# A four-layer model with a mixture of experts on one core: the router's lists by scatters instead of one-hot sums

## The chip, the cores and the metric

The kernel runs on one core of one Trainium2 chip. The metric is device microseconds for one execution. Five engines run side by side: PE (TensorE, matrix products), DVE (VectorE), ACT (ScalarE), POOL (GpSimd) and SP (SyncE, which here only starts DMAs). Each works through its own instructions in order and waits on semaphores for the others.

## The reference, cut to what matters

Four layers follow one another on 2048 rows (4 sequences of 512) of 512 features, each with a residual and a layernorm. Layers 1 and 2 (lightning attention, gated feed-forward) are not touched.

```python
# layer 3, the gated layer: q, k, v, g are four projections of x
g = sigmoid(x @ Wg.T + bg)
y = q * cumsum(k * v, axis=1) * g
x = layernorm(x + y)
# layer 4, the experts (E = 32, K = 8 chosen, the first 4 "primary")
logits = x @ gate_weight.T
probs  = softmax(logits)
top, idx = top_k(probs, 8);  w = top / sum(top)
sim[e, e] = 1
prim, sec = idx[:, :4], idx[:, 4:]
cand = sim[sec[:, :, None], prim[:, None, :]]
best = max(cand, -1);  best_primary = prim[argmax(cand, -1)]
new_sec = where(best < 0.5, sec, best_primary)
combine = sum(one_hot([prim, new_sec]) * w)          # rows x 32 weights
for e in range(32):
    g, u = split(x @ Wgu[e].T);  y += (silu(g) * u) @ Wd[e].T * combine[:, e]
x = layernorm(x + y)
```

## The kernel before

The rows are 16 tiles of 128, and four batches (b or q, 0 to 3) of four tiles. The program has these stages: attention, feed-forward (to 666.65 us in the trace), the **gated layer**, the **router's rest**, the **experts**, the final layernorm.

**The gated layer** is a loop over 16 steps `s`, with q = s // 4 and et = s % 4 (a quarter of the features). PE computes four projections of 12 matmuls each (k, v, q, g: `gate_proj(s, 0..3)`, L745), and between them `back(s-1)` (L761), which turns the last step's product round into bank 4. ACT copies the projections out (kC, then qC, then gC by a sigmoid); DVE makes k·v and its running sum `cumC`; POOL multiplies q by g (L1772) and then by `cumC` (L1777). After four steps a batch has its residual; DVE takes its mean and variance (`norms`), POOL makes 1/std and -mean/std (`shifts`, L1761 to L1767), ACT writes the normalised tile (`high_half`, L1541), POOL its low half (`x_low`, L1686), PE turns both round (`norm_transposes`, L768, through L551).

**The router** of batch q-1 runs beside the steps of batch q. PE computes the logits from the normalised, turned tiles (`logits`, L773, 48 small matmuls). DVE finds the eight best of 32 by softmax values (`choices`); PE turns the second choices round and multiplies by a block-diagonal similarity matrix (L789, L796); DVE picks, for each of the four first choices in turn, the similarity (L1212, L1213), then the new choices and the weights (`combine`); PE ranks each row among the rows of its expert (`ranks`, L799); DVE makes places of it (`places`, L1241).

**The lists.** The experts work on blocks of 128 rows, 159 blocks in all, and a block needs the list of its rows. For each batch and each of its 32 (tile, choice) pairs, DVE writes a one-hot of the column times the row's number (`one_hots`, L1266, up to 512 wide), POOL or ACT (in turns, L1786, L1561 with L1567) a one-hot of the place, and PE adds their product into bank 7 (`slot_sums`, L815). A short tail turns bank 7 into the table of blocks (`tables_ready`), and POOL starts the first gather of rows (L1819). The lists of batches 0 and 1 are made within the loop, those of 2 and 3 behind it.

**The experts.** POOL gathers a block's rows (L1819), PE multiplies, and POOL adds the result to memory by an indirect scatter (L1826); 159 of each. The change leaves this stage alone.

The order on every engine is the order in which the code is written; there is no scheduler.

## Time and profile before

| | us |
|---|---|
| time, median of 3 runs | 1586.79 (1586.19 to 1589.04) |
| the profiled execution's own time | 1585.89 |
| its span in the trace | 1584.0 |
| busy of the span: PE | 1448.3 (91%) |
| DVE | 952.9 (60%) |
| POOL | 776.5 (49%) |
| ACT | 732.3 (46%) |
| gated layer, to the end of its last projection | 666.65 to 871.20 |
| router's rest, to the first matmul of the experts | 871.20 to 955.90 |
| experts | 955.90 to 1570 |

PE is busy in nine tenths of nearly every fortieth of the span, except where the router's rest lies. So there are two kinds of place: those in which a microsecond on PE is a microsecond of time, and the router's rest, in which PE waits for others.

### The profile page before, as it was taken

Reading aid. Unit: us, or ns where it says so; the run is one execution under the profiler, and the core shown is the slowest. Engines: PE = TensorE matmul, PEld = TensorE weight load, DVE = VectorE, ACT = ScalarE, POOL = GpSimd, SP = SyncE. Lnnn points to the kernel's source line nnn. Section 1 sums busy time; section 2 is a strip of 40 time slices with the busy share of each in tenths; the row PEclk is TensorE's granted clock in tenths of the full one; section 3 lists DMA queues with packets and bytes.
Section 4 is the critical chain, followed back from the end, with each engine's and each line's share of the span. In section 5 each row is a group of like instructions: output and inputs, shape, how many; then the busy total and the mean of one; then the engine's idle time right before and its main releaser. Section 6 shows DMA issues by size and latency. Waiting matters only on the chain.

```text
span 1584.0 us, 33491 instructions
## 1 busy us (share of the span) xinstructions
PE 1448.3 (91%) x11191; PEld 820.2 (52%) x11192; DVE 952.9 (60%) x1858; ACT 732.3 (46%) x1326; POOL 776.5 (49%) x691
## 2 busy tenths in 40 slices
PE   5999999999999999999998358999999999999990
PEld 2566666544444444445454215666666666666650
DVE  7877777776757666634988883444444444444435
ACT  6544433555464645444446442444444444444443
POOL 3565544530010202044445536777777777777655
PEclk9999999999999999999999668999999999999995
DMA  6323111269776868531101444888989898876767
GB/s 242 107 81 107 27 40 26 77 219 315 238 255 232 265 222 268 179 139 54 55 3 54 158 165 93 185 183 166 202 177 206 177 196 186 162 108 96 177 76 230
DMA packets 102991, 243.45 MB, mean 154 GB/s; under 512 B 21481, under 2 KB 23049, under 8 KB 101904
## 3 DMA queue, kind: packets, MB, share of 16 engines
q1 hardware_dynamic: 67312, 183.08, 35.0%
q0 software_dynamic: 35616, 59.58, 23.0%
q8 instruction: 34, 0.56, 0.1%
q14 instruction: 29, 0.24, 0.0%
HBM read 158.92 MB, written 101.71 MB: 165 GB/s over the span
## 4 chain that ended last, share of the span: by engine, by line
PE 68%; DVE 16%; issue 6%; POOL 4%; ACT 3%; DMA 2%; SPq 0%; DVEq 0%; POOLq 0%; ACTq 0%
PE bank L894 20%; PE bank L915 11%; PE bank L562 8%; PE bank L706 6%; PE bank L712 6%; PE bank L735 6%; PE bank L885 5%; PE bank L904 2%; ACT ARENA L1395 1%; POOL ARENA L1695 1%; DVE ARENA L1032 1%; POOL ARENA L1690 1%; DVE ARENA L1266 1%; DVE ARENA L985 1%; PE bank L551 1%
## 5 line engine op out<-in xcount | busy, mean ns | idle before, releaser
L894 PE MATMUL bank<-ARENA,XT 128*128 x1908 | 364.2, 327 | 2.2 <-issue 1.1
L1826 POOL DMA_INDIRECT accs<-X,WA x159 | 252.5, 1588 | 98.8 <-issue 34.7
L894 PEld LDWEIGHTS bank<-ARENA,XT 128*128 128x128 f16 x1908 | 180.4, 98 | 124.2 <-issue 8.2
L1356 DVE COPY XT<-bank 128x1024 f16<-128x1024 f16 x159 | 109.9, 691 | 182.3 <-PE bank L885 181.1
L1819 POOL DMA_INDIRECT XT<-x_rows,WA x159 | 166.5, 1047 | 87.0 <-issue 39.8
L1395 ACT ACTIVATE ARENA<-ARENA 128x512 f16<-128x512 f32 (+2 forms) x128 | 89.3, 709 | 245.5 <-DVE ARENA L1114 134.1
L915 PE MATMUL bank<-ARENA,XT 128*128 x795 | 197.4, 379 | 0.9 <-issue 0.9
L1649 ACT ACTIVATE XT<-bank 128x192 f32<-128x192 f32 x159 | 52.5, 330 | 287.7 <-PE bank L894 287.7
L562 PE MATMUL bank<-XT,STG 128*128 128x512 f16 x640 | 151.8, 385 | 4.6 <-DVE ARENA L1160 4.3
L1677 POOL TENSOR_TENSOR rstd<-mv,mhalf 128x1 f32<-128x1 f32 x28 | 8.7, 309 | 258.2 <-DVE mv L964 258.2
L1395 ACT ACTIVATE XT<-bank 128x384 f16<-128x384 f16 (+2 forms) x207 | 125.7, 607 | 9.5 <-PE bank L551 9.0
L562 PE MATMUL bank<-WA,XT 128*128 128x512 f16 (+1 forms) x732 | 127.1, 327 | 2.4 <-DVE ARENA L1013 1.6
L735 PE MATMUL bank<-ARENA 128*128 128x512 f16 x512 | 121.0, 379 | 3.5 <-DVE ARENA L1120 3.4
L706 PE MATMUL bank<-XT,WA 128*128 (+1 forms) x512 | 122.6, 383 | 1.0 <-issue 1.0
L1366 DVE SCALAR_TENSOR_TENSOR XT<-bank,XT 128x192 f32<-128x192 f32 x159 | 66.4, 418 | 95.0 <-ACT XT L1649 91.8
L712 PE MATMUL bank<-XT,ARENA 128*128 (+1 forms) x512 | 121.7, 381 | 0.0
L1686 POOL TENSOR_TENSOR ARENA<-X,ARENA 128x512 f16<-128x512 f32 (+1 forms) x48 | 66.6, 1401 | 88.5 <-ACT ARENA L1395 88.5
L885 PE MATMUL bank<-ident,XT 128*128 128x128 f16 x1272 | 97.8, 220 | 5.5 <-DMA XT<-x_rows,WA 5.5
L915 PEld LDWEIGHTS bank<-ARENA,XT 128*128 128x128 f16 x795 | 71.7, 98 | 57.3 <-issue 1.4
L562 PEld LDWEIGHTS bank<-XT,STG 128*128 128x128 f16 x640 | 62.1, 99 | 74.8 <-DVE ARENA L1160 5.6
L885 PEld LDWEIGHTS bank<-ident,XT 128*128 128x128 f16 x1272 | 85.0, 98 | 25.7 <-issue 6.0
L1395 ACT ACTIVATE X<-bank 128x512 f32<-128x512 f32 x159 | 93.1, 586 | 2.1 <-PE bank L915 2.1
(245 smaller groups left out, 2369.6 us busy)
## 6 DMA issues: line engine op xcount, KB each, us to landing
w_scratch<-WA SPq DMA_DIRECT2D x64, 640.0 KB, 3.9
ARENA<-w_scratch SPq DMA_DIRECT2D x64, 640.0 KB
ARENA<-w_exp SPq DMA_DIRECT2D x48, 640.0 KB, 5.2
WA<-w_exp SPq DMA_DIRECT2D x16, 640.0 KB, 5.1
ARENA<-ARENA SPq DMA_DIRECT2D x64, 128.0 KB, 2.3
accs<-ARENA SPq DMA_DIRECT2D x20, 256.0 KB, 3.1
X<-x SPq DMA_DIRECT2D x4, 1024.0 KB, 6.6
ARENA<-wc SPq DMA_DIRECT2D x8, 512.0 KB, 6.0
```

Source lines behind the costliest of these rows:

```text
L562: mm = pe.matmul(dst, wa(a, k), wb(b, k), start=n == 0, stop=n == 3 * KD - 1)
L706: mm = pe.matmul(bank[0][:, :], Wg[:, n % KD, m * P:(m + 1) * P], XT[:, n // KD, n % KD, tk], start=n == 0, stop=n == 2 * KD - 1)
L712: mm = pe.matmul(bank[1 + m % 2][:, :], Wu[:, n % KD, m * P:(m + 1) * P], XT[:, n // KD, n % KD, tk], start=n == 0, stop=n == 2 * KD - 1)
L735: mm = pe.matmul(bank[4 + tt][:, :], fB[:, m % 2, a, tt * P:(tt + 1) * P], Wd[:, m, :], start=m == 0 and a == 0, stop=m == NM - 1 and a == 1)
L885: mm = pe.transpose(d[:, c * P:(c + 1) * P], xg[k.u % NG].bitcast(F16)[:, c * P:(c + 1) * P], ident16[:, :])
L894: mm = pe.matmul(d, xTb[k.u % 2][:, a * KD + kd, :], weights(sl, b, kd * 2 * DFF, 2 * DFF), start=(a, b, kd) == (0, 0, 0), stop=(a, b, kd) ...
L915: mm = pe.matmul(d, hT[k.u % 2][:, c, :], weights(sl, j, c0, DIM), start=n == 0, stop=n == 4)
L1356: dve.tensor_copy(xTb[k.u % 2].rearrange("p c n -> p (c n)"), bank[k.u % 2][:, :].bitcast(F16)).then_inc(xt_sb, 1)
L1395: return act.activation(dst, src, ACT.Copy, scale=scale)
L1686: pool.tensor_tensor(hl[:, 1, :], tile(t), hl[:, 0, :], ALU.subtract).then_inc(x_lo, 1)
L1819: pool.indirect_dma_start(xg[i % NG], None, xrows, bass.IndirectOffsetOnAxis(blkidx[:, i:i + 1], 0), bounds_check=TOK - 1, oob_is_err=Fals ...
L1826: pool.indirect_dma_start(accs, bass.IndirectOffsetOnAxis(blkout[:, i:i + 1], 0), yD[i % 8], None, compute_op=ALU.add).then_inc(y_out[i % ...
```

## The change

The functions keep their batches; what each engine does for a batch and where it stands is written anew.

- **Logits.** The normalised tiles are no longer turned round for the router (they still are for the first of the five groups, which feeds the gated layer itself). The scores are sums over the unnormalised residual: the layer's input times the gate weights (`input_logits`, before the third projection of a batch's step et = 1) plus, step by step, the layer's product times the gate weights (`layer_logits`, 4 float32 matmuls behind each `back`), all added up in bank 3. The mean is taken off with the gate weights' column sums (`gate_sums`, `csneg`); 1/std goes into the exponent of the eight best alone (`exponents`), so that the choice itself waits for no `shifts`.
- **Second choices.** First and second choices are both turned round (8 transposes, not 4), similarities are compared among the 32 experts with a priority matrix added (12 float32 matmuls, not 4), and DVE gets the new choices in nine operations.
- **Product.** POOL multiplies q by the running sum (one operation a step, L1800 of the new numbering), DVE multiplies by g (`product`).
- **Lists.** For batches 0 to 2 POOL writes each row's number to its place in a list in memory: `dispatch`, 32 indirect scatters a batch, each of 128 single float32 numbers, 96 in all. Batch 3 keeps 32 one-hots (DVE 53, ACT 11 pairs); two indirect gathers fetch the blocks' rows of the list (`listed`), and two matmuls add them in bank 7.
- **The rest.** The last batch's weights are made on POOL behind the scatters; constants come in two DMAs, the zeros of `accs` in four wide ones; four experts' weights are loaded within the loop.

```diff
@@ DVE @@
+            def product(s):
+                dve.wait_ge(gc_sb, s + 1)
+                dve.wait_ge(a1_ready, s + 1)
+                if s >= 2:
+                    dve.wait_ge(at_ready, s)
+                dve.tensor_tensor(aC[:, s % 2, :], a1C, gC, ALU.mult).then_inc(a_ready, 1)
...
+            def exponents(b):
+                dve.wait_ge(ln_rstd, 2 * NT + (b + 1) * TB)
+                step(dve.tensor_tensor(top8[:, :, 1:TOPK], top8[:, :, 1:TOPK], top8[:, :, 0:1].to_broadcast([P, TB, TOPK - 1]), ALU.subtract))
+                step(dve.memset(top8[:, :, 0:1], 0.0))
+                dve.tensor_tensor(top8, top8, rstd[:, :, 1:2].to_broadcast([P, TB, TOPK]), ALU.mult).then_inc(exp_in, 1)
@@ POOL @@
             def product(s):
-                pool.wait_ge(gc_sb, s + 1)
                 pool.wait_ge(qc_sb, s + 1)
-                pool.tensor_tensor(a1C, qC, gC, ALU.mult).then_inc(a1_ready, 1)
-                pool.wait_ge(a1_ready, s + 1)
                 pool.wait_ge(cum_ready, s + 1)
...
-                pool.tensor_tensor(aC[:, s % 2, :], a1C, cumC, ALU.mult).then_inc(a_ready, 1)
...
+                pool.wait_ge(a_ready, s)
+                pool.tensor_tensor(a1C, qC, cumC, ALU.mult).then_inc(a1_ready, 1)
+
+            def dispatch(b, lo, hi):
+                if lo == 0:
+                    pool.wait_ge(list_ready, b + 1)
...
+                for i in range(lo, hi):
+                    t = b * TB + i // TOPK
+                    pool.indirect_dma_start(slot_list, bass.IndirectOffsetOnAxis(places_i[b][:, i:i + 1], 0), pay[:, t:t + 1], None,
+                                            bounds_check=EXPERTS * TOK - 1, oob_is_err=False).then_inc(list_out, 16)
...
             for s in range(BATCH * KD):
                 q, et = s // KD, s % KD
...
+                if et == 0 and q >= 2:
+                    dispatch(q - 2, 14, 20)
+                if et == 1 and q >= 1:
+                    norm_shifts(q)
...
+                    dispatch(q - 2, 28, 32)
+                if et == 3 and q >= 1:
+                    dispatch(q - 1, 4, 10)
                 product(s)
                 if et == 0 and q >= 2:
...
+                    dispatch(q - 2, 20, 24)
+                if et == 1:
+                    low_halves(q)
+                if et == 1 and q >= 2:
+                    dispatch(q - 2, 24, 28)
+                if et == 2 and q >= 1:
+                    dispatch(q - 1, 0, 4)
+                if et == 3 and q >= 1:
+                    dispatch(q - 1, 10, 14)
+            dispatch(2, 14, 18)
+            norm_shifts(BATCH)
+            dispatch(2, 18, 24)
+            low_halves(BATCH)
+            dispatch(2, 24, 32)
+            pool.wait_ge(wts_ready, BATCH)
...
+            for g, rows in enumerate((P, NBLK - P)):
+                pool.indirect_dma_start(listed[0:rows, g, :], None, list_rows, bass.IndirectOffsetOnAxis(listidx[0:rows, g:g + 1], 0),
+                                        bounds_check=LISTROWS - 1, oob_is_err=False).then_inc(list_in, 16)
@@ PE @@
+            def layer_logits(s):
+                for tt in range(TB):
+                    mm = pe.matmul(bank[3][:, tt * EXPERTS:(tt + 1) * EXPERTS], aC[:, s % 2, tt * P:(tt + 1) * P], gw32[:, s % KD, :],
+                                   start=False, stop=s % KD == KD - 1 and tt == TB - 1)
...
                 gate_proj(s, 0)
-                if et == 1 and q >= 2:
-                    ranks(q - 2)
-                if et == 2:
-                    norm_transposes(q, 1)
+                if s == 2:
+                    norm_transposes(1)
                 gate_proj(s, 1)
...
+                if s == 1:
+                    gate_sums()
...
+                if et == 1:
+                    if q >= 1:
+                        choice_transposes(q - 1)
+                    input_logits(q)
+                if et == 2 and q >= 1:
+                    ranks(q - 1)
                 gate_proj(s, 2)
                 if s > 0:
                     back(s - 1)
...
+                    layer_logits(s - 1)
+                if et == 1 and q >= 1:
                     similarities(q - 1)
...
                 gate_proj(s, 3)
...
-                if et == 2 and q >= 1:
-                    logits(q - 1)
-                if et == 3 and q >= 2:
-                    slot_sums(q - 2)
@@ ACT, between kC and qC @@
                 if et == 1:
-                    for tt in range(TB):
-                        high_half(q, tt)
...
+                    if q >= 1:
+                        exponentials(q - 1)
+                    high_half(q, 0)
+                    high_half(q, 1)
+                    if q >= 1:
+                        second_copy(q - 1)
+                        first_copy(q - 1)
+                    high_half(q, 2)
+                    high_half(q, 3)
```

Three places of the order follow, before and after apart. The first is POOL's, in the last quarter of the gated layer (q = 3), before: L1686 are the low halves, L1772 and L1777 the product, L1786 the one-hots of places.

```order
L1686 TENSOR_TENSOR ARENA<-X,ARENA 128x512 [waits x_hi] x4
L1772 TENSOR_TENSOR ARENA<-ARENA 128x512 [waits qc_sb,gc_sb]
L1777 TENSOR_TENSOR ARENA<-ARENA 128x512 [waits at_ready,cum_ready,a1_ready]
L1786 TENSOR_SCALAR ARENA<-WA 128x128 [waits list_ready]
L1786 TENSOR_SCALAR ARENA<-WA 128x128 x7
```

The same place after: L1800 is POOL's product, L1809 the scatters (`dispatch`), L1790 to L1794 the `shifts` of one tile (four such threes follow one another, three of them behind these rows).

```order
L1809 DMA slot_list<-WA 81920x1 [waits list_ready]
L1809 DMA slot_list<-WA 81920x1 x9
L1800 TENSOR_TENSOR ARENA<-ARENA 128x512 [waits a_ready,cum_ready,qc_sb]
L1809 DMA slot_list<-WA 81920x1 x10
L1800 TENSOR_TENSOR ARENA<-ARENA 128x512 [waits a_ready,cum_ready,qc_sb]
L1809 DMA slot_list<-WA 81920x1 x4
L1790 TENSOR_TENSOR rstd<-mv,mhalf 128x1 [waits ln_stat]
L1792 TENSOR_TENSOR rstd<-rstd,mhalf 128x1 [waits g_step]
L1794 TENSOR_SCALAR rstd<-mv,rstd 128x1 [waits g_step]
```

Of the 8 one-hots a step nothing is left, and 24 scatters stand between a batch's list and the next `shifts`; 8 more follow the low halves.

POOL again, from the last `shifts` to the first gather of the experts, after (L1714 low halves, L1862 to L1870 the last batch's weights, L1874 the gathers of `listed`):

```order
L1809 DMA slot_list<-WA 81920x1 x6
L1714 TENSOR_TENSOR ARENA<-X,ARENA 128x512 [waits x_hi] x4
L1809 DMA slot_list<-WA 81920x1 x8
L1862 TENSOR_TENSOR WA<-WA 128x1024 [waits mask_ready,wts_ready]
L1865 TENSOR_TENSOR WA<-WA 128x512 [waits g_step]
L1867 TENSOR_TENSOR WA<-WA 128x4x64 [waits g_step]
L1870 TENSOR_TENSOR WA<-WA 128x128 [waits cw_out1,g_step]
L1874 DMA WA<-slot_list,WA 128x128 [waits list_out,list_ready]
L1874 DMA WA<-slot_list,WA 31x128
```

The gathers of the list stand behind all scatters and behind the weights.

PE at a batch's router work, before (step et = 3: L789 transposes of the second choices, L562 projections, L765 `back`, L796 similarities):

```order
L789 MATMUL bank<-ident,WA 128x128 [waits oh_ready]
L789 MATMUL bank<-ident,WA 128x128 x3
L562 MATMUL bank<-XT,STG 128x512 [waits qc_sb]
L562 MATMUL bank<-XT,STG 128x512 x9
L562 MATMUL bank<-XT,ARENA 128x512 x2
L765 MATMUL bank<-ident,ARENA 128x128 [waits res_added,a_ready]
L765 MATMUL bank<-ident,ARENA 128x128 x3
L796 MATMUL bank<-WA 128x128 [waits ohT_sb,bd_ready]
L796 MATMUL bank<-WA 128x128 x3
L562 MATMUL bank<-XT,STG 128x512 [waits gc_sb]
```

The same work after (now step et = 1: L808 transposes of both choices, L789 and L794 `input_logits`, L566 projection, L769 `back`, L799 `layer_logits`, L817 to L819 the first tile's similarities, three more tiles and then the g projection follow):

```order
L808 MATMUL bank<-ident,WA 128x128 [waits oh_ready]
L808 MATMUL bank<-ident,WA 128x128 x7
L789 MATMUL bank<-ARENA,ident 128x128 [waits zero_set,logit_sb]
L794 MATMUL bank<-WA,XT 128x32 x48
L566 MATMUL bank<-XT,STG 128x512 [waits qc_sb]
L566 MATMUL bank<-XT,STG 128x512 x9
L566 MATMUL bank<-XT,ARENA 128x512 x2
L769 MATMUL bank<-ident,ARENA 128x128 [waits res_added,a_ready]
L769 MATMUL bank<-ident,ARENA 128x128 x3
L799 MATMUL bank<-WA,ARENA 128x32 x4
L817 MATMUL bank<-WA 128x128 [waits ohT_sb,d_const,bd_ready]
L818 MATMUL bank<-WA 128x128
```

The similarities moved two steps ahead, into the step in which ACT also writes the high halves, and PE's last projection of that step stands behind them.

## Rows read from the trace of the kernel before

**Rows 1.** Busy us and instruction count of each engine by stage; clock, DMA, GB/s

```profile
666.65:871.20 204.55, 194.75 (x1180) 99.61 (x1179) 138.57 (x319) 97.48 (x173) 95.51 (x129) 0.98 0.18 63
871.20:955.90 84.70, 37.00 (x219) 19.17 (x218) 69.90 (x206) 35.82 (x88) 37.59 (x53) 0.63 0.46 155
955.90:1570.00 614.10, 583.88 (x4452) 364.02 (x4452) 258.67 (x674) 258.36 (x644) 428.96 (x338) 0.98 0.80 164
```

**Rows 2.** The chain of waits, at the tables' end: start us, us, what

```profile
940.22 8.04 PE bank L815 x24
...
950.81 0.33 DVE WA L1347
...
952.07 3.69 DMA XT<-x_rows,WA
...
955.90 1.03 PE bank L885 x8
```

**Rows 3.** Timeline of PE in the gated layer: start, us, line, operation

```profile
732.78 0.61 PE L551 MATMUL bank<-ident,ARENA 128*128 128x128 f16 x8
733.23 2.32 PE L562 MATMUL bank<-XT,STG 128*128 128x512 f16 x10
...
745.37 1.35 PE L562 MATMUL bank<-WA,XT 128*128 128x32 f16 x48
746.57 2.32 PE L562 MATMUL bank<-XT,STG 128*128 128x512 f16 x10
...
749.15 2.32 PE L562 MATMUL bank<-XT,STG 128*128 128x512 f16 x10
...
755.44 1.06 PE L796 MATMUL bank<-WA 128*128 128x128 f32 x8
756.34 2.32 PE L562 MATMUL bank<-XT,STG 128*128 128x512 f16 x10
...
862.50 0.86 PE L789 MATMUL bank<-ident,WA 128*128 128x128 f32 x4 [3.85 <-DVE WA L1199]
```

**Rows 4.** Timeline of PE in the attention, a float32 group 32 columns wide

```profile
309.02 1.12 PE L636 MATMUL bank<-ARENA 128*64 128x32 f32 x32
```

**Rows 5.** Timeline of POOL: shifts, low halves and products

```profile
831.24 0.19 POOL L1763 TENSOR_TENSOR rstd<-mv,mhalf 128x1 f32<-128x1 f32 x1 [0.20 <-DVE mv L964]
...
832.40 0.19 POOL L1763 TENSOR_TENSOR rstd<-mv,mhalf 128x1 f32<-128x1 f32 x1
...
835.81 4.50 POOL L1686 TENSOR_TENSOR ARENA<-X,ARENA 128x512 f16<-128x512 f32 x4
...
874.23 1.29 POOL L1772 TENSOR_TENSOR ARENA<-ARENA 128x512 f32<-128x512 f32 x1 [10.17 <-ACT ARENA L1618]
875.59 1.60 POOL L1777 TENSOR_TENSOR ARENA<-ARENA 128x512 f32<-128x512 f32 x1
...
884.78 5.47 POOL L1686 TENSOR_TENSOR ARENA<-X,ARENA 128x512 f16<-128x512 f32 x4
```

**Rows 6.** Timeline of ACT: high halves, a copy from PSUM, qC

```profile
863.39 0.60 ACT L1395 ACTIVATE WA<-bank 128x512 f32<-128x512 f32 x1 [0.76 <-PE bank L789]
...
867.47 0.69 ACT L1610 ACTIVATE ARENA<-bank,small 128x512 f32<-128x512 f32 x1 [3.47 <-PE bank L562]
...
881.44 0.81 ACT L1544 ACTIVATE X<-ARENA,rstd 128x512 f32<-128x512 f32 x1 [7.30 <-POOL rstd L1767]
...
882.82 0.80 ACT L1544 ACTIVATE X<-ARENA,rstd 128x512 f32<-128x512 f32 x1
```

**Rows 7.** Timeline of POOL: an indirect gather and an accumulating scatter

```profile
956.33 1.00 POOL L1819 DMA_INDIRECT XT<-x_rows,WA  x1 [0.30 <-issue]
...
1181.67 1.59 POOL L1826 DMA_INDIRECT accs<-X,WA  x1 [0.31 <-issue]
```

**Rows 8.** The gathers by their line: duration in ns, least, median, most

```profile
L1819 POOL DMA_INDIRECT XT<-x_rows,WA x159: 994/1048/1327, 952.1 to 1512.3; - x159
```

More of the change, by code:

```diff
@@ new lines, in ranks, with slot_sums @@
+                mm = pe.matmul(d, ones, before[b].rearrange("p t e -> p (t e)"), start=False, stop=not last)
+                if not last:
+                    mm.then_inc(rank_ready, 1)
+            def slot_sums():
+                for i in range(ROWS_B):
+                    if i % 3 == 0:
+                        pe.wait_ge(row_act, i // 3 + 1)
+                    pe.wait_ge(onehot_ready, i + 1)
+                    pe.matmul(bank[7][:, 0:NBLK], oneR[i], oneV[i][:, 0:NBLK], start=i == 0, stop=False)
@@ L1324, in _ @@
+            one_hots()
             eflat = eblk.rearrange("p g j -> p (g j)")
```

609 lines of the change are left out of this document (296 added, 313 removed).

## The prediction, made before the changed kernel was run

> **What bounds the kernel now.** I read the windows by stage first [rows 1]. In the gated layer PE is busy 194.75 of 204.55 us at a granted clock of 0.98; POOL has 95.51 us of work there, DVE 138.57. In the router's rest PE is busy 37.00 of 84.70 us, at a clock of 0.63, and DVE 69.90: this stretch is bound by waits. Then comes the expert stage, which the change leaves alone (583.88 of 614.10 us on PE). The chain of waits says what ends the rest [rows 2]: 24 `slot_sums` in 8.04 us, 0.335 each, which is the pace of DVE's one-hots; the table is complete at 950.81 + 0.33 = 951.14, the first gather is issued at 952.07 and its rows let PE begin at 955.90. So the question is when the tables are ready. Everything behind moves with them, whatever happened before.
>
> **What the change puts in.** Off PE, DVE and ACT go 96 of 128 pairs of one-hots; in their place POOL issues 96 indirect scatters in one row, shared out over the last nine steps and the rest. The order of POOL decides: the scatters of a batch stand before and behind the next batch's `shifts`, and the two gathers of the list behind all of them. I therefore count along POOL, with c for one scatter from start to start.
>
> *The first scatter.* Step 6 begins at 733.23 before, behind a tile's turning that now goes (732.78 to 733.23, -0.45) [rows 3]. On PE there come before it: two batches' input logits, priced as the 48 small matmuls that took 1.20 (745.37 to 746.57) and 0.1 for the zero matmul: 2.6; eight float32 choice transposes, about twice the four that take 0.5 to 0.86: 1.0; similarities, eight matmuls 128 wide at 0.22 (755.44 to 756.34 for four) and four of 32 columns. Of the 32-column float32 matmul the nearest row has 0.07 (1.12 us for 32 entries, two to a matmul) [rows 4], the 128-wide one is 0.22; I take 0.12, between them and nearer to the equal width. That is 2.3 for the similarities, 5 x 4 x 0.12 = 2.4 for `layer_logits` and 0.5 for `gate_sums` (bounds 1.4 less, 2.4 more in all). Two waits are new: the transposes' for DVE's choices, for which 3.85 is the largest before [rows 3] and 0 the least: 1.4; the similarities' for ACT's copies: 1.0. Sum -0.45 + 2.6 + 1.0 + 2.3 + 2.4 + 0.5 + 2.4 = 10.7, so step 6 begins at 744.0. Three projections of 2.59 (746.57 to 749.15), 0.4 for the ranks and 0.75 for qC [rows 6] give 752.9; the product before the scatter takes 1.36 (874.23 to 875.59) [rows 5]: 754.3.
>
> *A batch's round on POOL.* 32 scatters; four products of 1.36 = 5.44, where before there were two operations a step; shifts 4 x 1.14 = 4.56 (831.24 to 832.40 is one tile); low halves 4.50 for four, up to 5.47 [rows 5]. Once a batch POOL also stands still, and this is what the new order brings: in step et = 1 `shifts` release DVE's exponents (three short operations, 0.5), the exponential on ACT (0.3), then ACT makes two high halves, two copies and two more high halves before qC, and POOL's product waits for qC. That is 4 x 1.38 (881.44 to 882.82), 2 x 0.60, 0.7 for qC [rows 6] and 0.5 of hops: 8.7 us. PE waits in it too, the similarities standing before the last projection; it has slack there, because POOL is later. Round: 32c + 23.2. PE's own round without POOL would be 16 projections x 2.59 = 41.4, `back` and layer matmuls 4 x 0.9, input logits 1.3, transposes 1.0, similarities 2.3, ranks 0.4 and waits of 2.4: 52.4, against 64.8 on POOL for c = 1.30. So POOL is the bound from the first list on, and what else is added beside it costs nothing: DVE's product by g and its nine operations for the new choices (it had 66 us idle in this stage, and gives up 96 one-hots of 0.33 and the candidates), ACT's copies. If POOL isn't the bound, PE's list above is what they are behind.
>
> *The end.* From the third batch's first scatter: 32c + 1.36 + 4.56 + 4.50. Then the last batch's weights on POOL: 1024, 512, 256 and 128 wide, by 1.29 for 512 [rows 5] 2.6 + 1.3 + 0.6 + 0.3 = 4.8. Two gathers 1.3, landing 3.7 (952.07 to its end) [rows 2], the two matmuls and DVE's last two operations 1.2: 11.0. The 32 one-hots of the last batch (53 DVE operations of at most 0.33) run under the scatters.
>
> Tables at 754.3 + 2(32c + 23.2) + 32c + 10.4 + 11.0 = 822.1 + 96c.
>
> *The price of a scatter.* No plain scatter of single numbers is in the trace. The nearest row is the indirect gather: 1.00 busy and 0.30 to the next, 1.30 [rows 7], the same number of indices and issued by the same engine. The other neighbour is the accumulating scatter, 1.59 + 0.31 = 1.90. Below, I take 1.0: the busy time alone, should the gap go in a row of equal scatters without waits. I take c = 1.30: as with the gather, a scatter's POOL time should be that of 128 indices, not of what moves. Then the tables are ready at 946.9, 4.2 us before 951.14. Break-even is c = 1.34; with low halves of 5.47 in all three rounds, 1.31. The margin is thus a twentieth of a scatter, multiplied by 96.
>
> That this is tight shows in one row: beside a busy DVE the gathers' median is 1.048, the most 1.327, where those at the start take 1.00 [rows 7, 8]. 96 x 0.05 = 4.8 us would eat the gain. The Trainium skill has a rule that speaks against the change (page "SBUF — State Buffer", section "Who interferes with whom"): DVE's two-port operations lock GpSimd out while it writes descriptors, and a transfer of some 620 ns alone took some 3100 ns. By such a price the tables would be hundreds of microseconds late; the gathers' 1.327 at most, beside a DVE that copies in the expert stage, shows nothing of that size. The other rule that it has against this (page "DMA: Bandwidth & Descriptors", section "Rules for kernel authors") is that transfers under 64 KB are mostly overhead and should be made one; each scatter moves 512 bytes, and 96 of them are here, but the sum goes by POOL's row.
>
> *What is behind.* The expert stage is unchanged; its first experts' weights are now loaded earlier, the later ones wait for the last weights from POOL as before. I cost both at nothing, as expert 5 is used tens of microseconds later; a first gather landing 1 or 2 us later or earlier is in the range.
>
> The profiled execution took 1585.89 (span 1584.0 and 1.9 around it); 1585.9 - 4.2 = 1581.7. The median before lies 0.9 above that execution: **1582.5**.
>
> **Rivals.**
>
> A. *The scatters are cheap, and the rest shrinks.* With c = 1.0: 822.1 + 96 = 918. The floor is the dependent work without POOL: PE's loop ends near 871 as before (10.7 us later at step 6, with the slot sums, eight turnings and old waits gone behind it), then the last product, statistics, choices, transposes, similarities, new choices, ranks, places, 53 one-hot operations and the tables, some 40 to 43: 911 to 914. So 918 to 922, about 31 us less, less 2 for rounds in which PE is later: 1558. For: single numbers are less to describe than rows of 544 words. Against: the gather's time is the same in all of 159 cases but a few, 0.994 to 1.048, so it looks like a price per index.
>
> B. *A scatter costs what the accumulating one does.* The memory side is indexed for writing in both, and 1.90 is the only scatter in the trace. 822.1 + 182.4 = 1004.5, 53 later, and with longer waits on PE 3 more: 1643, slower. It decides from c = 1.34 on. Against: that scatter also adds, moves 512 floats a row, and half of its POOL time may come of that.
>
> C. *The scatter is a gather made longer by DVE.* In the gated layer DVE is busy two thirds of the time, with wide float32 operations and now the product too. At c between 1.40 and the gather's most, 1.33 + 0.30 = 1.63, the tables come 5 to 27 later: about 1600, slower. The contention rule cited above is its extreme.
>
> **How the numbers follow.** Forecast 0.47, A 0.30, B 0.12, C 0.11. A measurement of this kernel tells changes from 0.2% on, 3.2 us. The forecast's own range is 1573 to 1591 (c from 1.22 to 1.36, low halves 4.5 to 5.5, waits and layer matmuls as bounded). Of its 0.47, 0.25 is under 1583.6, 0.15 within 3.2 us of 1586.8, 0.07 above. With A: faster 0.55; same 0.15; slower 0.30. The range 1552 to 1612 takes in nearly all of A and most of C and leaves B out.
>
> **What would show it.** POOL's line for the scatters: 96, their busy time 1.00 to 1.05 and 0.30 between them; over 1.35 from start to start, C or B; about 1.0, A. Scatters without a gap from about 754 but for one stop of 8 to 9 us a batch, ended by ACT's qC. The gated layer on PE should grow from 204.6 to some 230 us, with waits before the similarities or for qC; the rest should shrink to some 55 us, and the chain there should run through POOL's scatters, the weights and the gathers of the list, not through `slot_sums`. Wrong would be a chain through DVE's one-hots or PE's similarities in the rest, or an expert stage (from the first gather's issue) that is more than 2 us longer or shorter.

## The result

The changed kernel takes 1602.53 us (median of four runs, 1599.30 to 1604.37), the kernel before 1587.67 beside it: ratio 1.0092, 95% interval 1.0070 to 1.0113. It is slower by 14.9 us. The forecast was 1582.5 and "faster"; the sign was wrong. (The times of one kernel move by some microseconds from execution to execution; the trace below is of the fastest of the four, 1599.30, so places are compared by their time in the trace.)

The windows by stage of the changed kernel (columns as in [rows 1]; the gated layer to its last projection, the rest to the first matmul of the experts, the experts):

```profile
666.65:897.31 230.66, 211.18 (x1288) 118.37 (x1286) 112.71 (x248) 70.44 (x102) 133.83 (x153) 0.95 0.29 81
897.31:967.39 70.08, 22.92 (x99) 14.77 (x99) 38.88 (x145) 16.13 (x36) 46.66 (x54) 0.53 0.43 95
967.39:1583.00 615.61, 584.54 (x4452) 364.21 (x4452) 258.21 (x674) 261.25 (x644) 426.76 (x336) 0.98 0.80 166
```

The gated layer grew from 204.6 to 230.7 us, as forecast (some 230), but the rest fell only to 70.1, where some 55 was forecast. POOL's busy time in the gated layer went from 95.5 to 133.8.

The scatters by their line (ns least, median, most), and POOL's timeline of the changed kernel at the places that the sum counted (start, us, idle before and what ended it):

```profile
L1809 POOL DMA_INDIRECT slot_list<-WA x96: 969/974/1984, 754.5 to 941.1; - x96
```

```profile
754.47 1.95 POOL L1809 DMA_INDIRECT slot_list<-WA  x1 [0.95 <-DVE WA L1279]
756.72 0.98 POOL L1809 DMA_INDIRECT slot_list<-WA  x1 [0.30 <-issue]
...
803.24 1.27 POOL L1800 TENSOR_TENSOR ARENA<-ARENA 128x512 f32<-128x512 f32 x1 [7.94 <-ACT ARENA L1646]
...
822.42 1.50 POOL L1809 DMA_INDIRECT slot_list<-WA  x1 [0.17 <-issue]
...
869.88 1.27 POOL L1800 TENSOR_TENSOR ARENA<-ARENA 128x512 f32<-128x512 f32 x1 [7.94 <-ACT ARENA L1646]
...
889.47 1.50 POOL L1809 DMA_INDIRECT slot_list<-WA  x1 [0.17 <-issue]
...
941.06 0.97 POOL L1809 DMA_INDIRECT slot_list<-WA  x1 [0.30 <-issue]
942.03 1.93 POOL L1862 TENSOR_TENSOR WA<-WA 128x1024 f32<-128x1024 f32 x1
...
954.74 1.12 POOL L1874 DMA_INDIRECT WA<-slot_list,WA  x1 [7.99 <-DMA slot_list<-WA]
...
963.00 1.03 POOL L1880 DMA_INDIRECT XT<-x_rows,WA  x1 [5.47 <-DVE WA L1381]
```

The first scatter came at 754.47 (forecast 754.3), and POOL stood still twice for 7.94 us, released by ACT's qC (forecast 8.7). A batch's round took 67.95 and 67.05 us from first scatter to first scatter (forecast 64.8). Then comes a wait that the sum did not hold: the gathers of the list had been next since 946.75, and POOL waited 7.99 us more, until the last scatters had landed (a transfer's landing is the moment at which its data has arrived and its semaphore says so). The chain of waits shows the same (start, us, what):

```profile
941.06 12.81 DMA slot_list<-WA
...
956.16 3.92 DMA WA<-slot_list,WA
960.12 0.80 PE bank L894 x2
...
963.00 4.25 DMA XT<-x_rows,WA
```

A second path is almost as late. DVE's one-hots of the last batch, which the prediction had under the scatters, begin when the last scatters are issued and end at 955.20:

```profile
940.38 0.41 DVE L1299 TENSOR_SCALAR STG<-WA 128x159 f16<-128x159 f16 x1
...
954.88 0.32 DVE L1299 TENSOR_SCALAR STG<-WA 128x159 f16<-128x159 f16 x1
```

So the first gather is issued at 963.00, against 952.07 before [rows 2]: 10.9 us later. From there to the end it is 634.5 us, against 632.0 (the spans less these). That the expert stage itself became slower isn't shown: in the fourteen variants below this stretch lies between 631.9 and 634.6, without a pattern that follows the edits.

### The profile page after: what moved, and what is told of

Read it like the earlier page. It is cut to its first block, busy times and chain, and to the rows that moved or that the text cites. A ratio compares the mean times of both kernels' runs of the same rounds, so it can differ in the third digit from the quotient of the medians.

```text
span 1597.5 us, 33188 instructions
## 1 busy us (share of the span) xinstructions
PE 1451.1 (91%) x11188; PEld 835.2 (52%) x11189; DVE 897.9 (56%) x1729; ACT 689.2 (43%) x1205; POOL 822.4 (51%) x714
## 4 chain that ended last, share of the span: by engine, by line
PE 40%; POOL 3%; DMA 2%; issue 2%; another core or an unknown queue 1%; DVE 1%; ACT 1%; POOLq 0%; SPq 0%; ACTq 0%; DVEq 0%
PE bank L913 20%; PE bank L934 11%; PE bank L904 5%; PE bank L566 3%; PE bank L923 2%; POOL slot_list L1809 2%; DMA slot_list<-WA 1%; DMA accs<-X,WA 1%; DVE bs L980 0%; PE bank L817 0%; DVE X L1414 0%; DMA X<-accs 0%; DMA XT<-x_rows,WA 0%; DMA WA<-slot_list,WA 0%
## 5 line engine op out<-in xcount | busy, mean ns | idle before, releaser
L566 PE MATMUL bank<-XT,STG 128*128 128x512 f16 x640 | 150.9, 383 | 0.0
L566 PE MATMUL bank<-WA,XT 128*128 128x512 f16 x540 | 121.6, 379 | 1.6 <-DVE ARENA L1032 1.6
L1809 POOL DMA_INDIRECT slot_list<-WA x96 | 104.5, 1088 | 28.7 <-issue 27.4
L1429 ACT ACTIVATE XT<-bank 128x384 f16<-128x384 f16 (+2 forms) x191 | 109.6, 574 | 12.7 <-PE bank L923 8.8
L1714 POOL TENSOR_TENSOR ARENA<-X,ARENA 128x512 f16<-128x512 f32 (+1 forms) x48 | 65.2, 1372 | 88.5 <-ACT ARENA L1429 88.5
L566 PEld LDWEIGHTS bank<-XT,STG 128*128 128x128 f16 x640 | 62.8, 101 | 71.0 <-issue 2.5
```

The source lines that it names most:

```text
L566: mm = pe.matmul(dst, wa(a, k), wb(b, k), start=n == 0, stop=n == 3 * KD - 1)
L1429: return act.activation(dst, src, ACT.Copy, scale=scale)
L1809: pool.indirect_dma_start(slot_list, bass.IndirectOffsetOnAxis(places_i[b][:, i:i + 1], 0), pay[:, t:t + 1], None, bounds_check=EXPERTS * ...
```

## What makes a scatter long

The median scatter took 0.974 us with 0.30 to the next, 1.27, less than the 1.30 taken. But their sum is 104.5 us, 11.3 more than 96 x 0.97. What a scatter takes above 0.97 is called its excess; it lies in about a quarter of them. One such piece of the changed kernel, DVE's timeline first, then POOL's:

```profile
769.81 0.69 DVE L1207 TENSOR_TENSOR ARENA<-ARENA 128x512 f32<-128x512 f32 x1 [5.58 <-POOL ARENA L1800]
...
772.90 1.22 DVE L1182 TENSOR_TENSOR_SCAN ARENA<-ARENA 128x512 f32<-128x512 f32 x1
775.14 0.69 DVE L1189 TENSOR_TENSOR ARENA<-bank,X 128x512 f32<-128x512 f32 x1 [1.02 <-PE bank L769]
```

```profile
769.88 1.50 POOL L1809 DMA_INDIRECT slot_list<-WA  x1 [0.17 <-issue]
771.69 0.97 POOL L1809 DMA_INDIRECT slot_list<-WA  x1 [0.30 <-issue]
772.97 1.94 POOL L1809 DMA_INDIRECT slot_list<-WA  x1 [0.30 <-issue]
775.21 0.97 POOL L1809 DMA_INDIRECT slot_list<-WA  x1 [0.30 <-issue]
```

Two scatters start while DVE works on two inputs in SBUF (the product by g, the running sum), and take 1.50 and 1.94. A third starts beside an operation as long whose first input is in PSUM (`bank`), and takes 0.97. Over all 96, laid against what DVE did at their start: 40 beside an idle DVE (or one that only clears), excess 0.1 us in all; 9 beside the product L1207, 3.9; 7 beside the running sum L1182, 3.4; 3 beside L1263 (1024 wide, two SBUF inputs), 3.0; 2 beside L1253 (512 wide, two SBUF inputs), 0.65; 10 beside two operations with a PSUM input, 0.04; 16 beside reductions, statistics and maxima, 0.03; the others have 0.2 together. Where a scatter comes right behind POOL's product it is always hit (7 times, 1.50 each): POOL's product releases DVE's product, and both start together. That comes of the change's own split.

One scatter is an exception and shows that the order of the two starts counts (DVE, then POOL):

```profile
781.54 1.29 DVE L1227 TENSOR_TENSOR WA<-WA 128x1024 f32<-128x1024 f32 x1
```

```profile
781.58 0.97 POOL L1809 DMA_INDIRECT slot_list<-WA  x1 [0.30 <-issue]
```

The operation has two SBUF inputs and had 1.25 us to go, and the scatter took 0.97 all the same; it had begun only 0.03 us behind it. The traces of four kernels have such a case (0.02 to 0.03 us, no excess), while at 0.05 us behind this same operation, with 1.17 to go, three others have 1.05.

The Trainium skill (page "SBUF — State Buffer", section "Who interferes with whom") has this rule: a DVE instruction with two SBUF inputs contends with a GpSimd instruction that reads SBUF, while a reduction never does. The trace agrees in both halves: 1.50 and 1.94 us beside two SBUF inputs, 0.97 beside reductions. The same section infers that such an operation doesn't hold up the writing of a DMA's descriptors. For these indirect scatters the measurement differs, and it decides.

## The experiments

All edits are to the changed kernel. "First gather" is the start of the experts' first gather of rows, 963.00 in the changed kernel, 952.07 before. Behind a time stand its ratio to the kernel before, measured beside it, and the 95% interval of that ratio. The times of different experiments were not measured side by side, so a few microseconds between their medians mean little; the first gather, from the traces, is the better measure.

**Expert 4's load behind the gathers of the list.**

```diff
-            load_expert(4)
             store_weights(3)
-            for e in range(5, NSLOT):
+            sp.wait_ge(list_in, 16 * 2)
+            for e in range(4, NSLOT):
```

> The changed kernel with one edit on SP's queue: expert 4's weights are loaded behind the gathers of the list (with experts 5 to 7), not ahead of the last batch's weights. In the changed kernel the last scatter landed 12.8 us after its issue and POOL waited 7.99 us for it. Theory L1 (the load takes the DMA engines from the scatters): the wait falls to 1 us or less, the gather of the list starts near 947.5 instead of 954.7, and DVE's one-hots, which end at 955.2, are then the last: tables some 4 to 5 us earlier, time about 1598. Theory L2 (the scatters themselves land slower than they are issued, so that a backlog has built up): the wait stays within 1 us of 8.0 and the time stays at 1602.

Measured: 1594.92 us (ratio to before 1.0056, 1.0040 to 1.0073), first gather 957.07.

```profile
947.16 1.11 POOL L1874 DMA_INDIRECT WA<-slot_list,WA  x1 [1.65 <-DMA slot_list<-WA]
...
957.07 1.03 POOL L1880 DMA_INDIRECT XT<-x_rows,WA  x1 [7.12 <-DVE WA L1381]
```

The wait fell from 7.99 to 1.65: most of the scatters' backlog came of the load of weights that was on the DMA engines. Not all: from the last scatter to the gather behind it there are still 7.34 us (939.82 to 947.16; 13.68 in the changed kernel). The gather of the list came 7.6 us earlier, of which 1.2 is an earlier last scatter, and the first gather of rows 5.9 earlier; then DVE's one-hots end last, as L1 said. The landing alone was thus worth less than 5 us of the tables' delay.

**Without the scatters of batches 0 to 2.**

```diff
-                for i in range(lo, hi):
+                for i in range(0):
...
-            pool.wait_ge(list_out, 16 * (BATCH - 1) * ROWS_B)
```

> The changed kernel without its 96 scatters (the lists of the first three batches stay empty, so the output is not the reference's; the number of blocks and gathers is the same). It shows what the rest of the change does. Theory P (POOL's scatters bind from the first list on): rounds of a batch fall from 67 us to PE's 52, the first gather of the experts is issued 38 to 48 us earlier, at 915 to 925, time 1555 to 1565. Rival Q (the new order of ACT, DVE and PE costs as much as the scatters do, which are hidden beside it): less than 15 us earlier, time above 1587.

Measured: 1550.41 us (0.9768, 0.9752 to 0.9785), first gather 915.79. Its windows, gated layer and rest:

```profile
666.65:870.00 203.35, 202.33 (x1290) 112.98 (x1288) 114.85 (x249) 70.36 (x102) 57.24 (x84) 1.00 0.26 92
870.00:919.00 49.00, 21.67 (x101) 13.58 (x100) 34.16 (x145) 16.21 (x36) 18.21 (x25) 0.59 0.46 154
```

All else in the change is worth 36 us, and PE has hardly a wait in the gated layer (202.33 of 203.35). The 96 scatters, with all that hangs on them, cost 47 us in the first gather and 52 in the medians. P is right, its time 5 us too high. The run also shows the loads' side: experts 2 and 3 were loaded, with their batch's weights stored behind them, from 798.98 to 811.22, 12.2 us; in the changed kernel, beside scatters, the same took from 810.14 to 846.50, 36.4 us. (The weights were ready at 820.8, so it was the loads that took the time.) So here the 512-byte scatters and the loads (1.3 MB for an expert) held each other up: the loads took three times as long, and in the run above the landing of the last scatter 6.3 us longer.

**25 more DVE operations beside scatters: two SBUF inputs, a reduction, a copy.**

```diff
+            def beside():
+                for _ in range(5):
+                    step(dve.tensor_tensor(spareD, onesC, zeros, ALU.mult))
...
+                    if et == 3 and q >= 1:
+                        beside()
                     product(s - 1)
+                if et == 1 and q >= 2:
+                    beside()
```

The two others have `tensor_reduce(spareD[:, 0:1], onesC, AX, ALU.max)` and `tensor_copy(spareD, onesC)` in that line.

> The changed kernel with 25 operations more on DVE in its idle time beside scatters (five ahead of the product in each step et = 3, five behind it in two steps et = 1): float32, 128x512, two inputs in SBUF, some 0.7 us each. Theory T1 (a scatter that starts while DVE works on two SBUF inputs waits for its end; 11 us of the 104.5 us that the scatters took were that): the scatters' sum grows by 7 to 17 us and the tables come as much later. Rival T2 (the long scatters, 1.3 to 1.98 us, come from the DMA queues or from the first scatter behind a POOL operation): the sum stays within 2 us of 104.5.

> The same as the kernel with 25 more two-input operations, but each is a reduction of one 128x512 float32 input in SBUF, about as long. T1: nothing is locked, the scatters' sum stays at 104 to 106 us. A theory T3, that any work on DVE slows POOL's scatters: the sum grows by 7 us or more here too. T2: 104.5 within 2.

> As the two kernels with 25 more DVE operations, but each is a float32 copy of one 128x512 tile in SBUF. In the changed kernel 40 scatters that started beside an idle DVE took 0.97 us each, and those beside a two-input operation 0.3 to 1.0 more; reductions added nothing. If only the second SBUF input counts, a copy adds nothing either: the scatters beside one take 0.97. If a copy takes both ports, the scatter waits for what is left of it, up to 0.4 us.

Measured: sums of 106.2, 101.2 and 104.6 us; times of one run each, 1598.28, 1603.29 and 1596.71, too few to rank. The sum with two-input operations rose by 1.7, which is inside T2's bound and far below my 7 to 17. One by one it looks otherwise: the 12 scatters that started beside an added two-input operation had 2.2 us of excess, the 8 beside an added reduction 0.04, the 8 beside an added copy 0.16. I had sized it wrongly: a scatter waits only for what is left of the operation (0.62 us left gave 0.53 of excess, 0.2 left gave 0.05 to 0.08), and only half of the added ones met a scatter's start, while others moved out of the way. As a test of the sum it was inconclusive; T3 (any work on DVE) fell. The copy was not tested: three of its 8 scatters began within 0.03 us of the copy's start, and the other five found 0.13 us of it or less. But two copies that were running when POOL's product began took 1.83 and 2.07 us instead of 0.43, so POOL's product does hold up a copy.

**POOL's shifts ahead of eight scatters.**

```diff
-                if et == 1 and q >= 1:
-                    norm_shifts(q)
                 product(s)
-                if et == 0 and q >= 2:
-                    dispatch(q - 2, 20, 24)
+                if et == 0 and q >= 1:
+                    norm_shifts(q)
+                if et == 0 and q >= 2:
+                    dispatch(q - 2, 20, 28)
...
-                if et == 1 and q >= 2:
-                    dispatch(q - 2, 24, 28)
```

> The changed kernel with POOL's order altered: a batch's shifts come in step et = 0, right behind the product, and the eight scatters that stood around them (20 to 27) follow the shifts, ahead of the product of et = 1. In the changed kernel POOL stood still for 7.94 us in each of these steps until ACT's qC. Theory P (POOL is the bound, and the chain shifts, exponents, high halves, copies, qC runs beside it): the two stops of 7.94 go to 1 us or less, POOL's rounds fall from 67 to 59 us, the tables come 14 to 17 us earlier, time 1586 to 1589. Rival (PE, which then has 52 us of work and waits in a round, becomes the bound, or the chain is only shifted): 0 to 6 us earlier, 1597 to 1602.

Measured: 1590.36 us (1.0026, 1.0009 to 1.0042), first gather 956.54. The products in question:

```profile
802.20 1.29 POOL L1800 TENSOR_TENSOR ARENA<-ARENA 128x512 f32<-128x512 f32 x1
814.46 1.26 POOL L1800 TENSOR_TENSOR ARENA<-ARENA 128x512 f32<-128x512 f32 x1 [0.54 <-ACT ARENA L1646]
...
863.41 1.28 POOL L1800 TENSOR_TENSOR ARENA<-ARENA 128x512 f32<-128x512 f32 x1
879.47 1.26 POOL L1800 TENSOR_TENSOR ARENA<-ARENA 128x512 f32<-128x512 f32 x1 [5.11 <-ACT ARENA L1646]
```

Both stops of 7.94 are gone, the first round is 62.1 us and the second 65.0; a new stop of 5.11 stands a step later. The last scatter ends 6.2 earlier and the first gather comes 6.5 earlier (14 to 17 expected). The medians differ by 12, but the two profiled executions by 6.5 (1592.78 and 1599.30), so no more than that is shown. P by the mechanism, less than half of its size.

**The order behind the loop.**

```diff
-            high_half(BATCH, 0)
             first_copy(3)
+            high_half(BATCH, 0)
...
-            exponents(3)
             dve.wait_ge(ohT_ready, 2 * BATCH - 1)
             dve.tensor_copy(...)
+            exponents(3)
...
-            dispatch(2, 18, 24)
             low_halves(BATCH)
-            dispatch(2, 24, 32)
+            dispatch(2, 18, 32)
```

> The changed kernel with the order altered behind the loop alone: ACT copies the first choices ahead of the first high half, DVE copies the second choices ahead of the exponents, and POOL does the low halves right behind the shifts, then the last 14 scatters in a row. Theory L1 (the landing of the scatters ends last, held up by expert 4's load): the similarities and DVE's one-hots come 3 to 5 us earlier, the scatters end when they did (942), so the tables move by less than 2 us; the load now starts 8 us earlier and the last landing may come earlier by as much of it, 0 to 5 us. Theory D (DVE's one-hots end last): 3 to 5 us earlier, about 1598.

Measured: 1595.30 us (1.0061, 1.0043 to 1.0079), first gather 958.78, 4.2 earlier. That is within both L1 and D. The trace is for L1: the load starts at 928.71 instead of 935.29, with 11 scatters to come instead of 5, POOL's wait for their landing is gone, and what ends last is the gather of the list, for which PE waits 2.00 us behind the last one-hot's product.

**The three together.**

> The three edits together: expert 4's load behind the gathers of the list, shifts ahead of eight scatters in each round, and the altered order behind the loop. If each takes away a wait of its own: 7.6 us for the load as measured, 14 to 17 for the shifts, 3 to 5 for the order: 1574 to 1578, faster than the kernel before. If they share one (the landing, or DVE's one-hots): 1580 to 1590.

Measured: 1587.67 us (1.0011, 0.9998 to 1.0024), first gather 949.79, 13.2 earlier than in the changed kernel; no difference from the kernel before. Alone they had brought 5.9, 6.5 and 4.2. Two of the three take away the same wait (the landing), so they don't add up. And DVE's one-hots now stand beside the last scatters:

```profile
932.60 0.25 DVE L1298 TENSOR_SCALAR STG<-WA 128x128 f16<-128x128 f16 x1 [1.04 <-issue]
932.77 0.32 DVE L1299 TENSOR_SCALAR STG<-WA 128x159 f16<-128x159 f16 x1
934.02 0.32 DVE L1299 TENSOR_SCALAR STG<-WA 128x159 f16<-128x159 f16 x1 [0.93 <-issue]
934.72 0.26 DVE L1298 TENSOR_SCALAR STG<-WA 128x128 f16<-128x128 f16 x1 [0.38 <-issue]
```

They idle for up to 1.09 us at the scatters' pace, which they don't do beside an idle POOL: here the scatter holds up DVE.

**Who multiplies.** First the whole product on POOL, then the whole of it on DVE, then the latter with the three edits:

```diff
 def product(s):                                  # on POOL, and nothing on DVE
     pool.tensor_tensor(a1C, qC, cumC, ALU.mult).then_inc(a1_ready, 1)
+    pool.wait_ge(gc_sb, s + 1)
+    pool.wait_ge(a1_ready, s + 1)
...
+    pool.tensor_tensor(aC[:, s % 2, :], a1C, gC, ALU.mult).then_inc(a_ready, 1)
```

> The changed kernel with its product whole on POOL again (q times the running sum, then times g), none of it on DVE: that part of the change undone alone. In the changed kernel the scatter right behind POOL's product took 1.50 us instead of 0.97 in nine cases, as DVE's product by g, released by it, read two SBUF inputs at that moment. Theory P (POOL is the bound): POOL gets 10 operations of 1.3 us more behind the first list, and waits for g in those steps in which it isn't late, and saves 9 x 0.4 to 0.5; tables 8 to 16 us later, time 1610 to 1619; the scatters' sum falls from 104.5 to about 100. Rival (the stops are long enough to take it in): within 3 us of 1602.

Measured: 1625.94 us (1.0253, 1.0237 to 1.0268), first gather 987.98, 25 later; the scatters' sum 101.1. The sum and the sign are as said; the cost is larger, as PE then waits for POOL (`PE bank L769 <- POOL`, 19.2 us).

```diff
 def product(s):                                  # on DVE, and nothing on POOL
-    dve.wait_ge(gc_sb, s + 1)
+    dve.wait_ge(qc_sb, s + 1)
+    dve.wait_ge(cum_ready, s + 1)
...
+    dve.tensor_tensor(a1C, qC, cumC, ALU.mult).then_inc(a1_ready, 1)
+    dve.wait_ge(gc_sb, s + 1)
     dve.wait_ge(a1_ready, s + 1)
```

> The changed kernel with the whole product on DVE, so that POOL has scatters, shifts and low halves alone and waits for no qC. Theory P: POOL loses 10 x 1.45 us behind the first list and two stops of 7.94 us (shifts wait for the statistics of et = 0 only): about 25 to 30 us earlier, if PE and DVE can follow; PE's own round is 52 us against POOL's 32 x 1.30 + 9.1 = 51, so some 20 to 28 us earlier with DVE collisions of 0.4 a step: time 1576 to 1584. Rival (PE, waiting for ACT's copies of the choices in step et = 1, then bounds): 5 to 15 us earlier, 1588 to 1598.

Measured: 1595.29 us (1.0056, 1.0041 to 1.0071), first gather 960.07.

> The three edits of order (expert 4's load, shifts ahead of eight scatters, the order behind the loop) and the whole product on DVE. With POOL out of the product the scatters should end some 15 us before the last batch's one-hots, which then run beside an idle POOL (0.27 us each, not 0.4): first gather 930 to 938 against 949.8 with the three edits alone, time 1567 to 1575, faster than the kernel before by about 1 %. If PE's slower clock behind its waits takes it back: 940 to 945, 1578 to 1582.

Measured: 1591.92 us (1.0032, 1.0019 to 1.0046), first gather 956.83, 7 us later than with the three edits alone. The first one's time is the rival's (7 us less than the changed kernel, 2.9 in the first gather), theory P failed; the second failed in both its ranges. POOL's timeline of the last one:

```profile
818.83 1.79 POOL L1813 DMA_INDIRECT slot_list<-WA  x1 [7.89 <-DVE WA L1283]
...
851.52 0.19 POOL L1794 TENSOR_TENSOR rstd<-mv,mhalf 128x1 f32<-128x1 f32 x1 [6.01 <-DVE mv L983]
...
886.12 1.80 POOL L1813 DMA_INDIRECT slot_list<-WA  x1 [8.77 <-DVE WA L1283]
```

POOL, with less to do, waits for DVE's lists and statistics, and a round is as long as before (66.6 and 67.3). "POOL is the bound" held for the order as it was, not for every order. What bounds now isn't the others' dependent work as such: without scatters (and with the product shared as in the change) PE needs 51 us for a round and has no wait in it. Beside scatters it is another picture (us, PE busy and so on as in [rows 1]; first a stretch of 51 us without scatters, then a round of this kernel):

```profile
752.00:803.00 51.00, 51.00 (x325) 28.68 (x324) 30.98 (x69) 17.23 (x25) 13.87 (x20) 1.00 0.26 89
```

```profile
752.22:818.83 66.61, 58.64 (x327) 32.84 (x326) 32.40 (x75) 17.35 (x25) 42.32 (x48) 0.90 0.23 53
```

As many matmuls take 58.64 us at a granted clock of 0.90, and gaps stand between matmuls of one row that wait for nothing which the profile shows ("issue"). From 750 to 895 us such gaps of more than 0.1 us add up to 12.5 us here, 15.9 without the edits of order and 3.4 in the changed kernel; there are none in the kernel before and none without scatters. The scatters thus have one more price, on PE. What PE waits for in these gaps no run shows.

**Two operands in PSUM.**

```diff
-                dve.scalar_tensor_tensor(kvC, bank[1][:, :], vb16[...], kC, ALU.add, ALU.mult).then_inc(kvc, 1)
+                dve.scalar_tensor_tensor(bank[1][:, :], bank[1][:, :], vb16[...], kC, ALU.add, ALU.mult).then_inc(kvc, 1)
-                dve.tensor_tensor_scan(cumC, onesC, kvC, 0.0, ALU.mult, ALU.add)
+                dve.tensor_tensor_scan(cumC, onesC, bank[1][:, :], 0.0, ALU.mult, ALU.add)
-                dve.tensor_tensor(aC[:, s % 2, :], a1C, gC, ALU.mult)
+                dve.tensor_tensor(aC[:, s % 2, :], a1C, bank[5][:, :], ALU.mult)
-                act.activation(gC, bank[5][:, :], ACT.Sigmoid, ...)
+                act.activation(bank[5][:, :], bank[5][:, :], ACT.Sigmoid, ...)
-                    pe.wait_ge(kvc, s)
+                    pe.wait_ge(cum_ready, s)
-                    pe.wait_ge(gc_sb, s)
+                    pe.wait_ge(a_ready, s)
```

> The changed kernel with two operands of DVE moved out of SBUF, nothing else: ACT writes the sigmoid g, and DVE k times v, in place into their PSUM banks, so that DVE's product by g and its running sum read one input in SBUF and one in PSUM. Instructions, their number and order stay. In the changed kernel 16 scatters started beside these two, 7.3 us longer in all than 0.97 each; those that started beside DVE operations with PSUM inputs took 0.97. Theory T1 (two SBUF inputs hold up the scatter): these 16 fall to 0.97 to 1.0 each, the scatters' sum from 104.5 to 97 to 98, the first scatter behind each product from 1.50 to about 1.0, tables 5 to 8 us earlier, time 1594 to 1598. T2 (the first scatter behind a POOL operation is long by itself; the scan's are chance): they stay at 1.50, sum 103 to 106, time 1602 within 3.

> The three edits of order (expert 4's load, shifts ahead of eight scatters, the order behind the loop; first gather at 949.8, 1587.7 us) with the two operands in PSUM. T1: the scatters' sum falls from 102.9 to 96 to 98, the first gather comes at 943 to 946, time 1581 to 1584, 0.2 to 0.3 % faster than the kernel before. If PE's waits bound the rounds by now: 948 to 950, 1586 to 1588.

Measured: the scatters' sum fell to 96.5 us, and a scatter that starts 0.53 us into the running sum to 0.97 (1.45 in the changed kernel, where its input was in SBUF). POOL's timeline, with DVE's line for this piece ahead of it:

```profile
761.86 1.22 DVE L1182 TENSOR_TENSOR_SCAN ARENA<-ARENA,bank 128x512 f32<-128x512 f32 x1
```

```profile
762.39 0.97 POOL L1809 DMA_INDIRECT slot_list<-WA  x1 [0.30 <-issue]
...
813.49 1.26 POOL L1800 TENSOR_TENSOR ARENA<-ARENA 128x512 f32<-128x512 f32 x1 [13.16 <-ACT ARENA L1646]
```

This settles T1's part on the scatters: the 10 of them that started beside the two operations (5 each) had no excess. Its times failed: they are 1606.51 (1.0112, 1.0095 to 1.0129), and with the three edits 1603.40 (1.0096, 1.0079 to 1.0113), first gathers 973.01 and 969.80. The stop for qC grew to 13.16, once. The edit does put in waits (PE's v projection now waits for the running sum, and that for POOL's product), and I took them for the cause. The trace doesn't bear that out. The first round took 76.04 us (67.95 in the changed kernel), the second, with the same waits, 67.66 (67.05); and ahead of the long stop DVE stood still between two of its own operations, the second of which waits for the first alone:

```profile
790.68 0.19 DVE L1224 FIND_INDEX8 WA<-WA 128x8 uint32<-128x32 f32 x1
803.63 0.18 DVE L1226 CAST WA<-WA 128x32 f32<-128x32 uint32 x1 [12.77 <-remote]
```

The exponents, the high halves and qC stand behind this stop. With the three edits it is 5.78 us at the same place, and 5.82 in the kernel with 25 added reductions; the changed kernel, the kernel before and the one without scatters have none. What ends it is not shown, and so neither is how much of the delay is the new waits' and how much this stop's.

**The three edits and g alone in PSUM.**

> The three edits of order (first gather 949.8, 1587.7 us) with g alone left in its PSUM bank; k times v stays in SBUF, so that PE's v projection waits for k times v, as before, and not for the running sum behind it. The trace of the run with both operands in PSUM had every first scatter behind a product at 1.01 us, and PE later, as its v projection waited through the running sum for POOL's product. Expected: the scatters' sum falls from 102.9 by 3 to 4 to about 99, PE has no new wait (the turning round ahead of the g projection waits for the same product already), first gather 946 to 947, time 1583 to 1585, 0.15 to 0.2 % faster than the kernel before. If PE waits for the g bank after all: 950 or later, 1588 or more.

Measured: 1581.82 us (ratio to the kernel before 0.9981, 0.9968 to 0.9995), first gather 946.73, 3.1 earlier than with the three edits. The six scatters beside the product have 0.1 us of excess instead of 1.7; the one behind a product, 1.50 in the changed kernel, now takes 1.01 (DVE, then POOL):

```profile
769.47 0.69 DVE L1207 TENSOR_TENSOR ARENA<-ARENA,bank 128x512 f32<-128x512 f32 x1 [5.57 <-POOL ARENA L1800]
```

```profile
769.54 1.01 POOL L1809 DMA_INDIRECT slot_list<-WA  x1 [0.17 <-issue]
```

The sum did not fall, it is 103.7: others met the running sum (8, 4.3 us) and the one-hots of choices (3, 2.5 us). So how much of the 3.1 us is the operand's is not shown. It is the one version with all its lists that beats both kernels, by 4.5 us (0.2%, twelve executions from 1580.30 to 1590.33) and some 20 us.

## Why the prediction was wrong

The sum was 822.1 + 96c with c = 1.30, tables at 946.9. They came at 962.20 (961.88 and 0.32 of DVE's last operation), 15.3 later. By its terms:

- **The first scatter**: 754.3 against 754.47, in part by luck. PE began step 6 at 743.30, not 744.0: neither of the two new waits (2.4) came there, and the added work took 1.7 more than said. POOL's product began at 752.25, not 752.9, and then POOL waited 0.95 us for DVE's list, which the sum didn't have.
- **c**: this step failed in size. An undisturbed scatter is 1.27 from start to start, 0.03 less than the gather's row, but 11.3 us of waiting, nearly all for DVE's two-input operations, make the mean 1.38: 7.4 us more than counted. I had named this as rival C, had its break-even at 1.34, and gave the gathers' 1.048 in the expert stage as its measure. Of those 159 gathers 61 start beside an idle DVE, 26 beside an operation with a PSUM input and 72 beside one with two SBUF inputs that lasts 0.22 us; all three groups are 0.05 above 1.00. So the row measured nothing of DVE, and none of its neighbours was long. In the gated layer the product and the running sum last 0.69 and 1.22. Shown by the two operands in PSUM (sum 104.5 to 96.5).
- **The stops for qC**: 8.7 each against 7.94. Right, 1.5 us less in all; shown by the shifts put ahead.
- **The last batch's weights**: 4.8 against 4.7. Right.
- **DVE's one-hots under the scatters**: this overlap failed. They began at 940.38, 0.7 us ahead of the last scatter, and ended at 955.20, so they alone kept the tables from 946.9. Had the scatters kept to the forecast's c, 7.4 us earlier, they would by an estimate still have ended near 947.8. With the load moved they end last, at a first gather of 957.07. It adds nothing to the 15.3 below only because the landing ended later still.
- **The landing of the last scatters**: this step was missing. The prediction set the gathers of the list right behind the weights, though their row in the order says that they wait for `list_out`. 7.99 us. Shown by moving expert 4's load, which I had cost at nothing "as expert 5 is used tens of microseconds later": I asked who needs the load, not what it shares the DMA engines with.
- **List gathers to tables**: 6.2 against 7.5, 1.3 more.

7.4 + 8.0 + 1.3 - 1.5 and small ones make the 15.3 along POOL. Rival A's floor (911 to 914 for the tables without POOL) was right: some 915 without scatters (first gather 915.79). Rival B was wrong: a plain scatter of numbers costs 0.97, not the accumulating one's 1.59. Rival C, at 0.11, was the mechanism of half of the miss, its c (1.40 at least) a little above the 1.38 measured. That its time (about 1600) is nearly right is luck, as the other half is the landing.

## What to carry over

Where an engine's queue is full, 0.08 us more for an instruction that stands there 96 times is enough to turn the sign (7.4 us against a margin of 4.2); read its price beside the same neighbours, and see which of these have two inputs in SBUF and how long they last. Asynchronous work has a second price, its landing: whoever waits for "all of them" waits also for what shares the DMA engines at that moment. Work that is said to run under other work needs its own start and end in the sum: the one-hots began when what should have hidden them was over. And before an edit is blamed for a longer wait, look whether the engine stood still where it had nothing to wait for.

## What I had not expected of the hardware

- A scatter of 128 single float32 numbers costs POOL 0.97 us, 0.03 less than a gather of 128 rows of 2176 bytes (1.00).
- The hold-up goes both ways: scatters wait for DVE's two-input operations (0.97 to 1.98 us), and DVE's float16 one-hots wait for scatters (gaps up to 1.09 with the three edits).
- Beside scatters PE and DVE have stops with no wait that the profile shows (PE 2.4 to 16.3 us from 750 to 895 us in every kernel with scatters, DVE up to 12.77 at once in a few). The kernel without scatters has none on PE and one of 1.08 us on DVE.
- A float32 operation with two SBUF inputs on DVE took 3.31 us instead of 0.69 beside POOL's low halves in the changed kernel:

```profile
928.16 0.69 DVE L1252 TENSOR_REDUCE WA<-WA 128x16 f32<-128x512 f32 x1
928.88 3.31 DVE L1253 TENSOR_TENSOR WA<-WA 128x512 f32<-128x512 f32 x1
```
